# Both layer norms of a convolutional-attention, Nystrom-attention and expert kernel: which engine writes the normalised rows

## The reference, cut to what matters

```
x = x + softmax(theta(x) phi(x)^T) g(x) W_out + b_out        # per sample, 32 channels inside
t = x
t = t + nystrom_attention(LN(t), w_qkv, w_out, b_out)        # 8 heads, 128 landmarks, 6 pinv steps
t = t + moe(LN(t), W_gate, W1, W2)                           # 16 experts, 2 per token, gelu
def LN(v): m = mean(v); s = var(v); return (v - m) / sqrt(s + 1e-5)   # over the 256 channels
```

## Time and profile before

| what | value |
|---|---|
| median of 3 runs | 1173.0 us |
| lowest and highest of them | 1167.71 and 1175.07 us |
| time of the profiled execution | 1169.51 us |
| its span, first to last instruction | 1167.9 us |
| granted TensorE clock, mean | 0.95 |
| PE busy | 987.8 us (85%) |
| DVE busy | 628.0 us (54%), 1586 instructions |
| ACT busy | 455.6 us (39%) |
| POOL busy | 326.5 us (28%), 356 instructions |
| chain that ended last | PE 55%, DVE 14%, issue 13%, DMA 10%, ACT 4%, POOL 2% |

### The profile page before, as it was taken

One profiled execution on the slowest core, in us unless ns is written; L12 is line 12 of the kernel. 1 busy time (PEld: TensorE's weight loads), 2 busy tenths in 40 slices (PEclk: granted clock), 3 DMA queues, 4 the chain that ended last, 5 costly groups with the idle time before them and its releaser, 6 DMA issues.

```text
span 1167.9 us, 21041 instructions
## 1 busy us (share of the span) xinstructions
PE 987.8 (85%) x6794; PEld 715.1 (61%) x6795; DVE 628.0 (54%) x1586; ACT 455.6 (39%) x1027; POOL 326.5 (28%) x356
## 2 busy tenths in 40 slices
PE   3999997899998799997899997148888888888886
PEld 2656654656654556654556654137777777777775
DVE  6766667667667667667766668962222222222221
ACT  3523364523364523364523364123333333333331
POOL 2220002230001230001220001244555555555553
PEclk8899999899999899999999999559999999999998
DMA  4000003000003000002000002982333333323330
GB/s 125 2 1 1 1 2 109 3 1 1 1 1 95 17 1 1 1 1 74 2 1 1 1 1 91 280 298 42 56 58 52 50 52 55 53 47 54 53 46 12
DMA packets 41266, 50.87 MB, mean 44 GB/s; under 512 B 10625, under 2 KB 32513, under 8 KB 41185
## 3 DMA queue, kind: packets, MB, share of 16 engines
q0 software_dynamic: 17344, 27.24, 12.1%
q1 hardware_dynamic: 23840, 22.56, 6.4%
HBM read 32.96 MB, written 18.78 MB: 44 GB/s over the span
## 4 chain that ended last, share of the span: by engine, by line
PE 55%; DVE 14%; issue 13%; DMA 10%; ACT 4%; POOL 2%; ACTq 0%; POOLq 0%; DVEq 0%
PE PS L557 10%; PE PS L489 9%; PE PS L882 6%; PE PS L741 6%; PE PS L518 6%; PE PS L873 5%; DMA out_dram<-low,row_of 5%; DMA low<-rows_scratch,token_of 5%; PE PS L649 2%; PE PS L630 2%; POOL out_dram L403 2%; DVE neg_max L1096 2%; PE PS L635 1%; ACT low L1043 1%; PE PS L609 1%
## 5 line engine op out<-in xcount | busy, mean ns | idle before, releaser
L882 PE MATMUL PS<-arena,low 128*128 x632 | 157.7, 393 | 36.9 <-ACT low L1043 25.0
L357 POOL TENSOR_SCALAR aggr<-aggr 128x1 f32<-128x1 f32 x64 | 14.6, 227 | 592.6 <-DVE aggr L1158 592.6
L403 POOL DMA_INDIRECT out_dram<-low,row_of x79 | 126.2, 1597 | 157.9 <-DVE low L1447 85.8
L873 PEld LDWEIGHTS PS<-low 128*128 128x128 f32 x1264 | 155.5, 194 | 4.1
L489 PE MATMUL PS<-ident,arena 128*128 128x128 f32 x1024 | 143.6, 286 | 16.3 <-ACT arena L964 9.7
L873 PE MATMUL PS<-low 128*128 128x128 f32 x1264 | 155.6, 277 | 0.0
L882 PEld LDWEIGHTS PS<-arena,low 128*128 128x128 f32 x632 | 114.3, 190 | 66.4 <-issue 53.6
L489 PEld LDWEIGHTS PS<-ident,arena 128*128 128x128 f32 x1024 | 121.0, 149 | 48.3 <-issue 37.8
L1096 DVE TENSOR_REDUCE neg_max<-PS 128x1 f32<-128x1024 f32 (+1 forms) x97 | 118.5, 1221 | 48.5 <-PE PS L557 45.1
L1043 ACT ACTIVATE low<-PS 128x512 f32<-128x512 f32 x79 | 47.2, 597 | 221.1 <-PE PS L873 202.4
L557 PE MATMUL PS<-arena 128*128 128x512 f32 x256 | 126.7, 597 | 0.0
(11 more groups left out here) (191 smaller groups left out, 1374.5 us busy)
## 6 DMA issues: line engine op xcount, KB each, us to landing
arena<-in_L_ffn_W_dram SPq DMA_DIRECT2D x32, 512.0 KB, 5.0
arena<-in_x_dram SPq DMA_DIRECT2D x4, 1024.0 KB, 8.4
rows_scratch<-arena POOLq DMA_DIRECT2D x4, 1024.0 KB, 6.7
out_dram<-t POOLq DMA_DIRECT2D x4, 1024.0 KB, 10.3
low<-rows_scratch,token_of POOLq DMA_INDIRECT x79
out_dram<-low,row_of POOLq DMA_INDIRECT x79
arena<-in_L_attn_w_qkv_dram SPq DMA_DIRECT2D x1, 768.0 KB, 4.7
arena<-in_L_attn_w_out_dram SPq DMA_DIRECT2D x1, 256.0 KB, 5.2
```

The lines of the kernel that those rows point to most:

```text
L403: pool.indirect_dma_start(out_rows, bass.IndirectOffsetOnAxis(ap=row_of[:, n:n + 1], axis=0), y_sb[:, n % 4, :], None, bounds_check=T - 1, ...
L873: mm = pe.matmul(PS[:, 2 + p, hc * P:(hc + 1) * P], w1_now[:, p, c * H + hc * P:c * H + (hc + 1) * P], xgT[:, p, c, :], start=c == 0, stop ...
L882: mm = pe.matmul(PS[:, 6 + p, 0:D], hT[:, p, c, :], w2_sb[:, bass.ds(e * (HC * D) + c * D, D)], start=c == 0, stop=c == HC - 1)
```

## The change

GpSimd, which makes the deviation, now also writes the normalised tile: `norm` moves from the vector queue to the gpsimd queue, directly behind the power, for both norms. The VectorE ends a tile with the moments. The semaphores `dev_ready`, `dev2_ready` and `xn_free` go, since nothing on another engine waits for the deviation, and the engine that writes `xn` has itself waited for the transfer that reads it. The chain `pool_steps` has a link more per tile (from the power to the norm).

```diff
-            pool.sem_inc(xn_free, 1)
-            pool_steps = Chain(sem("pool_steps"), 2 * NT)
-
-            def deviation(t, i):
+            pool_steps = Chain(sem("pool_steps"), 4 * NT)
+
+            def norm(row, t, i):
 
                 pool_steps.link(pool, pool.tensor_scalar(aggr[:, t, 2:3], aggr[:, t, 1:2], EPS_LN, None, ALU.add), i)
-                return pool.tensor_tensor(aggr[:, t, 3:4], aggr[:, t, 2:3], minus_half[:], ALU.pow)
+                pool_steps.link(pool, pool.tensor_tensor(aggr[:, t, 3:4], aggr[:, t, 2:3], minus_half[:], ALU.pow), i)
+                apart(pool, "pool")
+                return pool.tensor_scalar(xn[:, t, :], row, aggr[:, t, 0:1], aggr[:, t, 3:4], ALU.subtract, ALU.mult)
...
-                        deviation(t, i).then_inc(dev_ready, 1)
+                        norm(x1[:, t, :], t, i).then_inc(xn_ready, 1)
...
-                    deviation(t, i).then_inc(dev2_ready, 1)
+                    norm(t2[:, t, :], t, i).then_inc(xn2_ready, 1)
...
-                pool.sem_inc(xn_free, 1)
...
-                def norm(row, t):
-                    return dve.tensor_scalar(xn[:, t, :], row, aggr[:, t, 0:1], aggr[:, t, 3:4], ALU.subtract, ALU.mult)
...
-                        if s == 3:
-
-                            dve.wait_ge(xn_free, i + 1)
-                        if s >= 3:
-                            norm0(s - 3)
...
-                norm0(NT - 1)
...
-                        if s >= 3:
-                            norm1(s - 3)
-                norm1(NT - 1)
                 parts(i + 1, 0)
```

More of the change, by code:

```diff
@@ L249, in conv_attn_nystrom_moe_kernel @@
         x2_done = sem("x2_done")
-        xn_free = sem("xn_free")
-        dev_ready = sem("dev_ready")
-        dev2_ready = sem("dev2_ready")
         xn2_ready = sem("xn2_ready")
```

6 lines of the change are left out of this document (removed).

## The result

Four runs of the changed kernel took 1180.96 to 1189.18 us, median 1183.2; the kernel before took 1173.76 in the runs beside them. The ratio is 1.0108, with an interval of 1.0077 to 1.0139. The forecast of 1166 was wrong and the time lies above the range. It went the way of rival C: the new GpSimd instruction takes 1.23 us or more, not 0.50.

What follows compares the result with a forecast made beforehand. The chain of waits was PE 55%, DVE 14%, POOL 2%, with stage 1 bound by the VectorE and stage 3 by TensorE. Terms 0.52 + 0.27 + 0.22 + 0.45 = 1.46 us a sample, times 4 = 5.8, gave 1166 us; range 1157 to 1178.

Steps and rivals of the forecast that it cites:

- rival C: GpSimd too slow, deciding at d near 1.05 us; at d = 1.31 a loss, 1178 us in all; chance 0.17.
- The price d: Time of the new GpSimd norm instruction on one 128x256 input: 0.50 us, between 0.23 and 1.31.
- GpSimd's pace: Stage 1: a tile takes GpSimd 1.9 + d = 2.4 us against a 2.8 us step; free up to d near 0.9.
- The last norm: End of stage 1: norm ready at 416.35, before its readers; costs 0 up to d of 0.85, above that d - 0.85.
- Stage 1, the steps and step 8: Steps fall from 3.08 to 2.82 us, gaining 0.52 us a sample; copy L1084 in step 8 starts earlier, gaining 0.27.
- Stage 3, step 6: Copy L1303 follows the moments directly instead of the norm: gain 0.22 us a sample, between 0 and 0.29.
- Stage 3, its end: Conversion starts earlier while VectorE and GpSimd take turns: router product gains 0.45 us a sample, bounds 1.4 and -0.7.
- The later store: Store L383 goes out about 1.3 us later; only GpSimd's own queue waits for it: costed at 0.
- Rival D: More than the sum: shorter stand at stage 3's end keeps 2.4 GHz; about 10 us gained, 1161 or less; chance 0.20.

Runs made afterwards that it cites:

- e1: Kernel before plus eight extra GpSimd instructions a sample, of different forms and widths, that nobody waits for: 1174.4 us in one run, against 1168.9 to 1173.9 before.
- e4: Changed kernel with the second bias's eight additions put behind all eight norms in GpSimd's queue: ratio 0.9996 to the kernel before.
- e10: Changed kernel with the next load of x held back until the next sample's first moments: ratio 1.0091 to the kernel before.
- e2: Only the second norm on GpSimd, the first left on the VectorE as in the kernel before: ratio 0.9985 to that kernel.
- e8: Norms divided: GpSimd writes tiles 0, 1, 4 of the first and 0 to 6 of the second, VectorE the rest; biases behind: 0.9936 to the kernel before.
- e9: e8 with the load of x and the store of t2 both held back into the next pass: 1154.06 us, ratio 0.9856 to the kernel before.
- e5: Changed kernel with GpSimd writing only 128 of the 256 columns of each normalised row, the rest zeroed once: ratio 0.9961 to the kernel before.
- e3: Only the first norm on GpSimd, the second left on the VectorE as in the kernel before: ratio 1.0070 to that kernel.
- e6: Kernel before with the next load of x held back until the next sample's first moments: ratio 0.9964 to the kernel before.
- e11: e8 with only the next load of x held back until the next sample's first moments: ratio 0.9903 to the kernel before.
- e7: e6 with the store of t2 also held back behind the next sample's first moments, and biases behind the norms: ratio 0.9971 to the kernel before.

## Why the prediction was wrong, point by point

- **The price d: this step failed.** 0.50 us forecast, 1.23 and 1.29 measured, near the upper end of 1.31 that I had worked out and set aside. The reason for the choice, half the reads of the nearest row, was an assumption about an operation that no row had; e1 shows that the form of the instruction makes most of the price.
- **GpSimd's pace: wrong by the price alone.** Forecast 1.9 + d a tile, measured 3.00 = 1.77 + 1.23. The mechanism is that of rival C, and e4 takes the queue away with the price unchanged. That C's formula gives 5 x (3.13 - 2.8) = 1.65 us of queue for the measured d, near the measured 1.85, is in part luck: the tile took 0.13 less than taken, and the moments came 2.66 us apart and not 2.8, because the change itself shortens the stage. With both measured it is 5 x (3.00 - 2.66) = 1.7, and 0.17 by which the third tile was already late. The pace was free up to d of about 0.9.
- **The last norm: wrong by the price alone.** d - 0.85 = 0.38 by the prediction, 0.60 measured in e4, or 0.75 where the biases are late in both.
- **Stage 1, the steps and step 8: right.** 2.82 us forecast, 2.81 measured; the four stretches lost 0.9 each, the two terms together said 0.79.
- **Stage 3, step 6: wrong and small.** -0.22 a sample forecast; the stretch is 0.07 longer. In the changed kernel, in e4 and in e10 the copy has an idle time that the trace gives to nobody, here in the VectorE's timeline of the second sample:

```profile
356.94 0.18 DVE L1155 BATCH_NORM_AGGREGATE aggr<-stats 128x2 f32<-128x6 f32 x1 [0.15 <-DVE stats L1153]
357.42 0.42 DVE L1282 COPY arena<-PS 128x256 f32<-128x256 f32 x1 [0.29 <-issue]
```

  In e2, e8 and e9 the stretch is 0.3 shorter (116.26 to 116.29 us against 116.57), as forecast: there the copy starts 0.10 us behind the moments and not 0.48. In e5, whose VectorE queue has one instruction more ahead of the loop, the idle time stands one instruction earlier, at L1156. That speaks for a place in the queue and against the instruction itself, but no run tests it alone; what makes it stays open.
- **Stage 3, its end: right in size, half for the wrong reason.** -0.45 a sample forecast, 0.47 measured at the router's transposes; the copy starts 0.48 earlier (0.34 forecast), the product itself only 0.24. I had two errors that cancel. The norm is 0.73 to 0.8 dearer than taken; and the VectorE's subtractions do not stand behind it, as the turns of the earlier trace rows had made me count. With half the price (e5) the place gives 0.9 a sample on average (0.6 to 1.1).
- **The later store: not free.** I looked for who waits on the semaphore and found nobody. The transfers themselves stand in the way of TensorE's restart, as far as the packet records go by way of the instruction packet that lands late. The longer stands cost 2.5 us of the sum above. The recovery behind them adds 1.9, but it varies from pass to pass in the kernel before too. No run holds the store back in the changed kernel itself.
- **The clock.** Rival D saw only the gain of a shorter stand, and that came: the second router product took 1.88 us in all four samples, where the kernel before has 3.56 and 3.38 in two of them, at the lower clock. It was worth 0.2 us at most, since the subtractions end last there, as D had said against itself. But the change made a longer stand elsewhere, at `turn(6)`, and in two of four samples the clock fell behind it: 1.71 and 2.74 us (15.09 and 16.12 against 13.38), 4.4 in all.
- **Rival C as a number.** By its own formula C at d = 1.23 is +5 us. The profile gave +12.6 up to the end of the loop. The 7.4 between are a net of large terms. On the one side stand the clock (4.4), the restart with its recovery (4.4), a wait at `turn(6)` 1.7 longer than the formula's 8.1 and step 6, which lost 0.3 where 0.9 was to be gained (1.2). On the other stand the end of stage 3, which gained 1.9 where the formula with d = 1.23 loses 1.1 (3.0), and the start and the steps (1.2). C's chance of 0.17 was too low for a price bounded by 0.23 and 1.31 and decided at 1.05, and its time of 1178 too low because I priced no second effect of a TensorE that stands.

Shown by runs: the price (e1), the first norm as the place (e2, e3), the queue (e4), the sign decided by the price (e5), transfers at the restart (e6, e11 against e9). Read from all traces together: the clock falls behind the stand of 2.4 us. It fell in 8 of the 12 samples that have the stand (2 of 4 in the changed kernel and in e3, 4 of 4 in e10) and in none of the 40 samples of the ten other kernels, where TensorE waits 0.54 us or less at that place; e4 takes the stand away by the order of GpSimd's queue alone, and the clock holds. Why it falls in some samples and not in others is open, and so are the idle time of step 6 and the two lengths of the recovery.

## What to carry to other kernels

Before an elementwise operation moves to GpSimd, its exact form should have a measured price; a one-input instruction with scalar operands is not cheaper than a two-input addition but 1.7 times as dear (1241 against 727 ns). A helper engine that serves a pipeline is judged by its whole cycle per tile against the step: a cycle of 3.00 us against moments that come 2.66 apart on average is not seen at the first tiles and is a queue of 1.85 us at the eighth, so the work that nobody waits for (here the biases) belongs behind the work that somebody does, and only the tiles with slack should move. And a transfer that nobody waits for may still be in the way where the loop starts again: look at what the DMA queues of the kind "instruction" do there.

## What the runs showed of the hardware that I had not expected

- GpSimd's `tensor_scalar` at 128x256 takes 0.85 us with one constant and 1.24 with two per-row operands, 3.3 ns a column, while the copy takes 0.40.
- GpSimd and the VectorE beside each other need not take turns by whole instructions: two subtractions of the VectorE (1.53 us, 1.38 alone) ran inside one GpSimd norm (1.73 us, 1.23 alone). The Trainium skill's rule (SBUF — State Buffer, "Who interferes with whom") that the first holds the ports to its end fits and not this pair.
- TensorE's restart at a new pass of the loop takes 3.6 to 4.1 us when no data is under way (e6, e7, e9) and up to 6.8 when the DMA engines are full. In 39 of 39 stands it comes 1.49 to 1.59 us after the landing of a 16 KB packet of queue 8, kind "instruction", and with the DMA engines full that packet starts up to 4.2 us after the transposes and not 1.2.
- Behind a restart the time to the first moments is 11.4 to 11.8 us (21 of 39) or 12.6 to 13.4 (18 of 39), in the same kernel, from one pass to the next. In all 39 the clock is at its lower level (0.50) when TensorE restarts, and what differs is when it comes back: 2.8 to 4.5 us after the restart in the short ones, 8.0 to 9.6 in the long ones. Two windows of the kernel before (TensorE's busy us, granted clock, DMA share, GB/s), 5.7 us behind its first restart and 5.1 behind its second:

```profile
212.00:214.00 2.00, 2.00 (x15) 0.50 0.00 0
388.00:390.00 2.00, 1.80 (x25) 1.00 0.00 0
```

  What decides it is open.
- Once a sample an instruction of the VectorE can wait 0.3 to 0.4 us for nothing that the trace shows, at a place that stood one instruction earlier in e5, which has one more ahead of the loop.
